# A graph layer on Trainium2: GpSimd's gathers and scatters unrolled, the scatters four groups behind, 18 dense rows a step

## The reference

```python
h = jnp.maximum(_layernorm(x, axis=-1), 0.0)
z = jnp.concatenate([h[src], h[dst], edge_attr_32], axis=-1)
m = jax.nn.sigmoid(z @ W_f + b_f) * jax.nn.softplus(z @ W_s + b_s)
message = jax.ops.segment_sum(m, src, num_segments=100000)
mean = jnp.mean(message, axis=0)
var = jnp.mean((message - mean) ** 2, axis=0)
normed = (message - mean) * jax.lax.rsqrt(var + 1e-5) * gamma + beta
return x + h + normed
```

## Time and profile before

| | us |
|---|---|
| median of 3 runs | 1177.55 |
| lowest and highest | 1175.6, 1177.74 |
| profiled execution, span | 1163.4 |
| stage one, last scatter issued until | 940.49 |
| first table load of stage two | 947.58 |

### The profile page before, as it was taken

One profiled execution on the slowest core, in us unless ns is written; L12 is line 12 of the kernel. 1 busy time (PEld: TensorE's weight loads), 2 busy tenths in 40 slices (PEclk: granted clock), 3 DMA queues, 4 the chain that ended last, 5 costly groups with the idle time before them and its releaser, 6 DMA issues. The chain is left out here.

```text
span 1163.4 us, 11837 instructions
## 1 busy us (share of the span) xinstructions
PE 734.6 (63%) x3189; PEld 547.1 (47%) x3189; DVE 714.0 (61%) x1188; ACT 502.6 (43%) x1144; POOL 730.0 (63%) x596
## 2 busy tenths in 40 slices
PE   0687786766758676766857676666857100089976
PEld 0476664655646564645636564555647100033322
DVE  1377656465655647565564756556477328999956
ACT  0477454554545354454535445453547027700000
POOL 5767878888887878888787888878766620000000
PEclk9787655666575566666566566766566555589989
DMA  7995344333434333232332323233333249749998
GB/s 275 389 362 136 64 101 76 82 79 78 98 59 99 68 71 62 43 62 41 63 43 59 61 43 61 41 63 43 61 54 46 14 163 399 327 178 386 426 428 365
DMA packets 77417, 161.95 MB, mean 139 GB/s; under 512 B 39663, under 2 KB 46159, under 8 KB 68687
## 3 DMA queue, kind: packets, MB, share of 16 engines
q1 hardware_dynamic: 22575, 80.90, 19.1%
q0 software_dynamic: 40768, 19.31, 16.1%
q10 hardware_dynamic: 14048, 61.46, 13.4%
HBM read 93.87 MB, written 67.75 MB: 139 GB/s over the span
## 5 line engine op out<-in xcount | busy, mean ns | idle before, releaser
L327 POOL DMA_INDIRECT xg<-in_x_dram,gidx x392 | 380.3, 970 | 131.5 <-issue 114.9
L339 POOL DMA_INDIRECT msgs_dram<-comb,target x196 | 348.6, 1779 | 78.1 <-issue 57.3
L408 DVE TENSOR_REDUCE row_sum<-xg 128x24 f32<-128x1536 f32 (+2 forms) x53 | 86.4, 1631 | 320.1 <-DMA xg<-in_x_dram,gidx 320.1
L550 ACT ACTIVATE sq<-xc 128x1536 f32<-128x1536 f32 (+2 forms) x53 | 73.4, 1384 | 285.1 <-DVE xc L416 259.7
L685 PE MATMUL ps_z<-ident,xc 128*128 128x128 f32 x196 | 52.6, 421 | 180.6 <-DVE xc L465 180.6
L711 PE MATMUL ps_c<-msg,same 128*128 128x64 f32 x980 | 155.3, 331 | 4.5 <-ACT same L596 4.5
L711 PEld LDWEIGHTS ps_c<-msg,same 128*128 128x128 f32 x980 | 154.9, 250 | 4.6 <-ACT same L596 4.6
L698 PEld LDWEIGHTS ps_v<-w_e,ea_t 128*128 128x128 f32 x392 | 102.2, 320 | 70.9 <-issue 70.9
L698 PE MATMUL ps_v<-w_e,ea_t 128*128 128x128 f32 x392 | 128.6, 430 | 0.0
L685 PEld LDWEIGHTS ps_z<-ident,xc 128*128 128x128 f32 x196 | 34.3, 211 | 190.9 <-DVE xc L465 190.9
L695 PE MATMUL ps_v<-b_row,ones 1*128 1x512 f32 x98 | 96.5, 1083 | 38.4 <-ACT z_t L573 38.4
(11 more groups left out here) (87 smaller groups left out, 968.0 us busy)
## 6 DMA issues: line engine op xcount, KB each, us to landing
m_buf<-msgs_dram SPq DMA_DIRECT2D x38, 1024.0 KB, 20.2
msgs_dram<-zeros ACTq DMA_DIRECT2D x16, 1536.0 KB
xg<-in_x_dram SPq DMA_DIRECT2D x48, 512.0 KB, 3.6
out_dram<-m_buf ACTq DMA_DIRECT2D x21, 1024.0 KB, 9.9
y_spill_dram<-y_kept ACTq DMA_DIRECT2D x19, 512.0 KB, 3.0
y_kept<-y_spill_dram SPq DMA_DIRECT2D x9, 1024.0 KB, 30.0
xg<-in_x_dram,gidx POOLq DMA_INDIRECT x392
msgs_dram<-comb,target POOLq DMA_INDIRECT x196, 3.3
```

The costliest lines, as they stand in the source:

```text
L327: pool.indirect_dma_start(xg[:, slot, 2 * j + c, :], None, x, bass.IndirectOffsetOnAxis(ap=gidx[:, g.slot(UNROLL), c, j:j + 1], axis=0),). ...
L339: pool.indirect_dma_start(msgs, bass.IndirectOffsetOnAxis(ap=target[:, g.slot(UNROLL), j:j + 1], axis=0), comb[:, g.slot(UNROLL), j, :], N ...
```

## The change

- GpSimd's program is written out completely: 49 steps without a loop. The gathers read their indices from the loaded table `ids`; the tile `gidx`, its copy on VectorE and the semaphores `staged` and `gathers_begun` are gone.
- Steps 7, 8 and 9 each scatter two groups, the later steps one, so that step n from 10 on scatters group n - 4. Four groups are left after the last gather.
- 18 dense rows a step instead of 16: 44 steps carry them, from step 5 to step 48, the step of the last gather. After it the other engines run 3 steps (`TAIL`) without dense rows. The layer norm instructions cover 26 rows.
- 16 groups of dense rows are spilled (288 rows) instead of 19 (304 rows). The step at which y changes from spilled to kept falls inside an iteration, which is written out on VectorE and ScalarE (`TURN`).
- The equality tiles `same` are packed: 10 of 128 columns instead of 16. The zeroing keeps its 16 rows.

```diff
-BULK = 16
+BULK = 18
+NODE_GROUPS = -(-N_ROWS // BULK)
-SKEW = 4
-STEPS = GROUPS + SKEW
+SKEW = 5
+STEPS = NODE_GROUPS + SKEW
+TAIL = 3
-SPILL = 19
-ACC_LAG = 7
+SPILL = 16
+ACC_FIRST, ACC_LAG = 7, 4
+ZERO_ROWS = 16
...
-            def gather(g):
-                slot = g.slot(SLOTS)
+            def gather(n):
+                if n >= SLOTS:
+                    pool.wait_ge(centred, n - SLOTS + 1)
                 for j in range(TILES):
                     for c in range(2):
                         pool.indirect_dma_start(
-                            xg[:, slot, 2 * j + c, :], None, x,
-                            bass.IndirectOffsetOnAxis(ap=gidx[:, g.slot(UNROLL), c, j:j + 1], axis=0),
-                        ).then_inc(gathered[slot], 16)
+                            xg[:, n % SLOTS, 2 * j + c, :], None, x,
+                            bass.IndirectOffsetOnAxis(ap=ids[:, c, n * TILES + j:n * TILES + j + 1], axis=0),
+                        ).then_inc(gathered[n % SLOTS], 16)
...
-            for u in range(2 * UNROLL):
-                step(Group(u // UNROLL, u % UNROLL))
-            with pool.Fori(2, ITERS) as it:
-                for u in range(UNROLL):
-                    step(Group(it, u))
-            for u in range(1 + ACC_LAG):
-                step(Group(ITERS, u))
+            pool.wait_ge(ids_loaded, 96)
+            begun = 0
+            for n in range(GROUPS):
+                gather(n)
+                if n == ACC_FIRST:
+                    pool.wait_ge(table_zeroed, 16 * (ZERO_PARTS + 2))
+                for _ in range(0 if n < ACC_FIRST else min(2, n - ACC_LAG + 1 - begun)):
+                    accumulate(begun)
+                    begun += 1
+            for n in range(begun, GROUPS):
+                accumulate(n)
...
-            def stage_indices(g):
-
-                dve.tensor_copy(gidx[:, g.slot(UNROLL), :, :],
-                                ids[:, :, bass.ds(g.n * TILES, TILES)]).then_inc(staged, 1)
+            def stage_sources(g):
+
...
-            for u in range(STEPS - LAST + 1):
+            for u in range(1 + TAIL):
                 step(Group(ITERS, u), False)
...
-        same = sb("same", [P, TILES, TILES, P])
+        same = sb("same", [P, PAIRS[TILES], P])
```

More of the change, by code:

```diff
@@ L40 @@
 N_REST = NODES - P * N_ROWS
-LAST_ROWS = N_ROWS - BULK * LAST
+NODE_GROUPS = -(-N_ROWS // BULK)
+LAST_ROWS = N_ROWS - BULK * (NODE_GROUPS - 1)
 UNROLL = 6
 ITERS = LAST // UNROLL
-SKEW = 4
-STEPS = GROUPS + SKEW
+SKEW = 5
+STEPS = NODE_GROUPS + SKEW
+TAIL = 3
 SLOTS = 3
-SPILL = 19
-KEPT_ROWS = (GROUPS - SPILL) * BULK
-ACC_LAG = 7
+SPILL = 16
+KEPT_ROWS = (NODE_GROUPS - SPILL) * BULK
+ACC_FIRST, ACC_LAG = 7, 4
 ZERO_PARTS = 16
 ZERO_AHEAD = 4
+ZERO_ROWS = 16
 DUMP = (TILES + 1) * P
 assert ALL_TILES == TILES * GROUPS and ITERS * UNROLL == LAST and UNROLL % SLOTS == 0
-assert 0 < LAST_ROWS < BULK
-assert (SPILL + 1 + SKEW) % UNROLL == 0
+assert 0 < LAST_ROWS < BULK and STEPS == GROUPS
+TURN = (SPILL + SKEW) // UNROLL
+PAIRS = [b * TILES - b * (b - 1) // 2 for b in range(TILES)] + [TILES * (TILES + 1) // 2]
+assert 1 <= TURN < ITERS
 S_BLK = 32
@@ L174, in stage_one @@
         upto = sb("upto", [P, P])
-        zeros = sb("zeros", [P, BULK * F])
+        zeros = sb("zeros", [P, ZERO_ROWS * F])
         w_z = sb("w_z", [P, 2 * F])
@@ L179, in stage_one @@
         own = sb("own", [P, UNROLL, TILES])
-        gidx = sb("gidx", [P, UNROLL, 2, TILES], I32)
         xg = sb("xg", [P, SLOTS, ROWS, F])
@@ L307, in load @@
                     load_edges(g)
-            run_groups(sp, load, SKEW)
+            run_groups(sp, load, 0)
         @block.gpsimd
@@ L339, in accumulate @@
                     pool.indirect_dma_start(
-                        msgs, bass.IndirectOffsetOnAxis(ap=target[:, g.slot(UNROLL), j:j + 1], axis=0),
-                        comb[:, g.slot(UNROLL), j, :], None, compute_op=ALU.add,
+                        msgs, bass.IndirectOffsetOnAxis(ap=target[:, n % UNROLL, j:j + 1], axis=0),
+                        comb[:, n % UNROLL, j, :], None, compute_op=ALU.add,
                     ).then_inc(accumulated, 16)
[L344 to L350, removed]
-                    pool.wait_ge(table_zeroed, 16 * (ZERO_PARTS + 2))
-                if g.back(ACC_LAG).exists():
-                    accumulate(g.back(ACC_LAG))
-            for u in range(2 * UNROLL):
-                step(Group(u // UNROLL, u % UNROLL))
-            with pool.Fori(2, ITERS) as it:
-                for u in range(UNROLL):
-                    step(Group(it, u))
-            for u in range(1 + ACC_LAG):
-                step(Group(ITERS, u))
+            pool.wait_ge(ids_loaded, 96)
[3 more added lines that the diff above has]
+                if n == ACC_FIRST:
+                    pool.wait_ge(table_zeroed, 16 * (ZERO_PARTS + 2))
+                for _ in range(0 if n < ACC_FIRST else min(2, n - ACC_LAG + 1 - begun)):
[3 more added lines that the diff above has]
+                accumulate(n)
             pool.wait_ge(accumulated, 16 * ALL_TILES)
@@ L489, in step @@
                 if g.back(-1).exists():
-                    stage_indices(g.back(-1))
+                    stage_sources(g.back(-1))
                 if in_steps(g.back(1)):
@@ L512, in _ @@
                 step(Group(0, u), True)
-            first_kept = (SPILL + 1 + SKEW) // UNROLL
-            with dve.Fori(1, first_kept) as it:
+            with dve.Fori(1, TURN) as it:
                 for u in range(UNROLL):
                     step(Group(it, u), True)
-            with dve.Fori(first_kept, ITERS) as it:
+            for u in range(UNROLL):
+                step(Group(TURN, u), TURN * UNROLL + u <= SPILL + SKEW)
+            with dve.Fori(TURN + 1, ITERS) as it:
                 for u in range(UNROLL):
                     step(Group(it, u), False)
-            for u in range(STEPS - LAST + 1):
+            for u in range(1 + TAIL):
                 step(Group(ITERS, u), False)
@@ L643, in _ @@
                 step(Group(0, u), True)
-            first_kept = (SPILL + 1 + SKEW) // UNROLL
-            with act.Fori(1, first_kept) as it:
+            with act.Fori(1, TURN) as it:
                 for u in range(UNROLL):
                     step(Group(it, u), True)
-            with act.Fori(first_kept, ITERS) as it:
+            for u in range(UNROLL):
+                step(Group(TURN, u), TURN * UNROLL + u <= SPILL + SKEW)
+            with act.Fori(TURN + 1, ITERS) as it:
                 for u in range(UNROLL):
                     step(Group(it, u), False)
-            for u in range(STEPS - LAST + 1):
+            for u in range(1 + TAIL):
                 step(Group(ITERS, u), False)
@@ L710, in combine @@
                     for b in range(j + 1):
-                        pe.matmul(ps_c[:, j, :], same[:, b, j, :], msg[:, b, :], start=(b == 0), stop=(b == j))
+                        pe.matmul(ps_c[:, j, :], same[:, PAIRS[b] + j - b, :], msg[:, b, :], start=(b == 0), stop=(b == j))
                 last = g.known and g.n == LAST
```

26 lines of the change are left out of this document (12 added, 14 removed).

## The result

The changed kernel took 1199.56 us (median of 4 executions, 1195.17 to 1205.03), the kernel before 1177.05 us beside it: ratio 1.0201, 95% interval [1.018, 1.0222]. It is slower, as forecast, but by 22.5 us instead of 6.3, and outside the range. Whether it is more than 2% slower, the interval leaves open.

A forecast was written before the change was run, and what follows sets the result against it. GpSimd was taken to bound stage one, never waiting there. Terms -9.0 + 30.9 - 25.3 + 10.7 - 1 = +6.3 on 1163.4 gave a span of 1169.7, plus 14.15: 1183.9 us; range 1172 to 1190.

The forecast's parts named there:

- part 2: Start of stage one: indices from ids, without gidx copy or staged wait, remove GpSimd waits; -9.0 us, range -9.5 to -6.
- the last one of the sum: Whole kernel: the 14.15 us between profiled span and median of runs carries over, 1169.7 to 1183.9 us.
- 1 unrolled: GpSimd's written-out program: unrolled steps already took as long as looped ones, so worth 0.
- 3 four behind: Steps 7 to 9 and tail: doubled scatter groups cost +30.9, the shorter tail gives -25.3; net +5.6 us.
- 4 18 rows: Steps 8 to 47: longer centring holds each third scatter 0.27 us longer; +10.7 us, bounds 0 and 16.
- 5 stage two: Packed same tile, spills and stage two's returning blocks: -1 us, between -4 and +1.
- Rival (b): Doubled steps and tail: groups cost 9.6 each and TensorE runs at full clock; 1178.9 us, no change, chance 0.14.
- Rival (a): Third scatter of each step: its hold does not grow, the 10.7 us drop out; 1173.2 us, faster, chance 0.20.
- Rival (c): Fourth scatter or first gather newly held by the y_kept sum, up to 1.26 us a step; 1234 us, chance 0.03.
- Rival (d): First scatter: the table's zeros are late and it waits 3 us; 1187 us, chance 0.07.

The follow-up runs named there:

- after_third: The changed kernel, unaltered, run a third time, beside the kernel before at 1168.5 us: 1168.81 us, ratio 0.9998.
- ids_no_wait_again: Second run of the kernel before, written out, with gathers reading ids, no gidx copy and no staged wait: ratio 0.9913.
- before_look: The kernel before, unchanged, profiled beside the third run of the changed kernel: 1167.24 us, span 1165.5.
- unroll_only: The kernel before with GpSimd's program written out for all steps and nothing else: ratio 0.9993 to the kernel before.
- lag4_second: Second run of the kernel before with indices from ids, no staged wait and scatters 4 behind, 16 dense rows: ratio 0.9929.
- The PSUM experiments: ids_no_wait with row_sum and row_rstd in PSUM (0.9862 of the kernel before), and with row_sum alone in PSUM (0.9879).
- no_wait_psum_rows: ids_no_wait with row_sum and row_rstd in PSUM, the message sum not kept (output lacks the right mean): 0.9862 of the kernel before.
- after: The changed kernel as first measured and profiled, beside the kernel before at 1177.05 us: 1199.56 us, ratio 1.0201.
- rows18_lag7: The changed kernel with gather groups 1 to 7 waiting on own_staged and scatters 7 behind again: 1.0062 of the kernel before.
- ids_no_wait: The kernel before, written out, gathers reading ids, without gidx copy and staged wait, 7 behind, 16 dense rows: ratio 0.9905.
- the early waits: The changed kernel with one wait put back, gather groups 1 to 7 waiting on own_staged: 1.0091 of the kernel before.
- after_pauses: The changed kernel with a wait for the previous gathers' landing ahead of gather groups 4 to 7: 1.0188, later 1.0167, of the kernel before.

## Why the prediction was wrong, and where it was right

**The step that failed is part 2, and with it the last one of the sum.** Part 2 said of GpSimd's new wait, on the centring of three groups back: it "is met some 13 us before it is asked for", and of the zeroed table: "the zeros have landed by then". In the result's profile gather steps 6 and 7 stand in that wait for 11.59 and 5.50 us, and the first scatter waits 18.82 us for the zeros and starts at 120.80 instead of 90.7.

The last step of the sum was "the median of the runs is 1177.55, 14.15 more, and I carry that over". In every later execution the own time is its span plus 1.7 (1199.08 and 1197.4, 1167.24 and 1165.5). So the profiled execution took about 1165.1 us, 12 us less than the runs it stood beside. By this, and by its trace (under what stays open), it was of the kind seen in five sessions, which I call the first kind; the times were of the other kind. That difference is no constant that can be carried over: it is a condition with which a change may interact, and this one did.

Part 2 (-9.0) was worked out from a trace of the first kind. There it is right: in `after_third` the centring is done 13.6 to 14.8 us before each of gather steps 3 to 7 begins (forecast 13), step 7 starts at 78.43 (forecast 79), and step 8 of `ids_no_wait_again` is 10.1 earlier than in `before_look`. On the other kind the wait that part 2 removes is replaced by a longer one, for TensorE's signals, and then by one for the zeros: the first scatter at 120.80 instead of 89.60, 31.2 us. Of these the wait for the zeros is 18.82 less 0.30. The other 12.7 are the two waits of 11.59 and 5.50 less their usual gaps (16.5), less 3.8, because in the third session some gathers were longer (up to 2.22). The last scatter ends 31.0 later (975.54 against 944.58), the span is 27.6 longer. By the medians the changed kernel is 30.8 us slower on that kind (1199.56 against 1168.81) and the kernel before 8.5 (1177.05 against 1168.54), and the difference of the two is the 22 us measured.

**The other steps, on chips of the first kind.** Counted at the end of the last scatter, one execution each:

| part | from, to | forecast | measured |
|---|---|---|---|
| 1 unrolled | before, `unroll_only` (ratio) | 0 | 0.9993 |
| 2 no wait | 938.68 to 931.17 | -9.0 | -7.5 |
| 3 four behind | 931.17 to 933.01 | +5.6 | +1.8 |
| 4 18 rows | 933.01 to 944.58 | +10.7 | +11.6 |
| 5 stage two | 226.8 to 225.2 after it | -1 | -1.6 |
| sum of spans | 1165.5 to 1169.8 | +6.3 | +4.3 |

The kernels are `before_look`, `ids_no_wait_again`, `lag4_second` and `after_third`. The medians of the third session differ by 0.3 us, with an interval of -2.3 to +1.8, while these single spans differ by 4.3; the times of one kernel scatter by some 8 us (1163.3 to 1171.6 in the third session), and stage two alone took 221.2 us in `lag4_second` and 225.2 in `after_third`, so each row is known to a few us only. By the medians part 2 gave 10.3 and 10.7 us (third and first session), and parts 3 to 5 together cost 10.6 where the forecast had 15.3. On this kind the change is "same", not "slower": that the forecast had the sign right is luck, since it came true only by the stall.

Part 2 in the table: of the 10.1 us at gather step 8, 2.0 go again in step 8 itself, where the fourth scatter takes 3.08, and step 8 20.42 instead of 18.40. That hold was not in the forecast. The first gather starts 0.9 earlier (5.06 against 5.95), not 0.2.

Part 3 was right in its mechanism and mis-sized in one term, the price of a second scatter group in a step. The windows of POOL in `lag4_second`, steps 7 to 9 and 10 to 47:

```profile
77.76:164.29 86.53, 65.26 (x49) 0.70 0.48 114
164.29:867.80 703.51, 564.51 (x456) 0.60 0.33 63
```

Steps 7 to 9 take 86.53 against 59.25 without the doubled groups (`ids_no_wait_again`): 27.3 for three groups, 9.1 each, not 10.3 (bounds 9.6 and 11). The forecast took the group price from the tail and added it to steps of 18.5; undoubled, steps 7 and 8 are 20.25 and 20.42, with holds that the doubled ones lack in part. The tail gives back 24.7 (25.3 forecast). In the changed kernel (`after_third`) steps 7 to 9 take 31.3, 28.4 and 28.3, where the forecast had 28 to 30 each. Rival (b) had this direction.

Part 4 held. The same windows of `after_third`:

```profile
78.43:166.46 88.03, 65.82 (x48) 0.64 0.44 105
166.46:879.66 713.20, 574.20 (x456) 0.60 0.33 65
```

713.20 less 703.51 is 9.7, or 0.255 a step where 0.27 stood. One step of the changed kernel (first profile), against the earlier trace rows:

```profile
529.51 1.89 DVE L410 SCALAR_TENSOR_TENSOR xc<-row_sum,xg 128x1664 f32<-128x1664 f32 x1
530.14 2.67 POOL L343 DMA_INDIRECT msgs_dram<-comb,target  x1 [0.30 <-issue]
531.32 1.88 DVE L459 SCALAR_TENSOR_TENSOR xc<-xc,row_rstd 128x1664 f32<-128x1664 f32 x1
533.12 1.54 POOL L343 DMA_INDIRECT msgs_dram<-comb,target  x1 [0.30 <-issue]
533.38 1.36 DVE L472 TENSOR_TENSOR y_kept<-xc,xg 128x1152 f32 x1 [0.18 <-DVE xc L459]
```

L410 had 1.26 left at 530.14; less 0.12 that is 1.14, and the scatter is 1.13 longer than the fourth. The same rule gives the length of all 41 such third scatters within 0.03 us, in this profile and in `after_third`; the mean third scatter took 2.71 us in both (forecast about 2.75, before 2.50). The PSUM experiments show the cause, which the prediction had only argued: with one SBUF input in place of two the same instruction holds nobody. Rival (a) is refuted. Rival (c) did not come in the changed kernel, but its mechanism is real: in `no_wait_psum_rows` the y_kept sum holds a gather (829.36, above). The Trainium skill ("SBUF — State Buffer", Who interferes with whom) puts all three on one shared port; these runs agree. The same section tells of a probe in which `tensor_tensor`, the form of the y_kept sum, did not stall a DMA; here it holds 35 gathers of `no_wait_psum_rows` by the rule above, within 0.03 us, and the measurement decides. Rival (d) was the right place (zeros and first scatter) with the wrong price, 18.5 us instead of 3, and only where the stall is.

**What stays open.** What makes a chip, or a session, of the second kind, and why TensorE's signals come late there. The traces have a mark of it: those with the stall keep 4,766 to 6,026 landing events of DMAs (five traces, the changed kernel's first among them), all others, the one of before that the forecast was read from among them, 12,974 to 13,170. Waits put down to "remote" stand only in the five, in the waits view of the first one from 30 to 125 us:

```profile
ACT spl L574 <- remote: 33.9, 1, 33.9
...
DVE not_later L426 <- remote: 28.8, 1, 28.8
...
ACT ea_t L566 <- remote: 12.9, 2, 6.9
```

Whether fewer kept events are a cause of the late signals or another effect of the same thing, no run tells.

The record of semaphores has a second mark. Of 245 signals of TensorE in stage one, every one stands within 0.02 us of the end of its matmul in each of the fifteen traces without the stall. In the five with it, 82 to 123 are more than 0.5 us late, and 70 to 110 of these belong to gather step 10 and later, late by up to 6.5 us. So the signals go on being late to the end of stage one; from step 10 on it costs GpSimd nothing (steps of 18.80 us against 18.77 in `after_third`). Some signals are missing from the record in these five; they are not counted. The guess that they come only when GpSimd stops issuing gathers has this for it: 220 of the 506 late signals belong to matmuls that end while a gather group is being issued, but only 19 arrive in such a time, though it is half of stage one; the others come while GpSimd scatters or pauses. The first long waits of `after` end 4.5, 1.7 and 1.7 us after GpSimd stops, those of `rows18_lag7` 2.9, 1.7 and 1.2 us. Against a simple form of it: other signals come on time in the midst of gathers, in the same traces, as they do in `ids_no_wait` throughout. So the guess is not shown. With pauses it was never tried on such a chip. Nor is there a profile of the kernel before there, so where it loses its 8 us is not known. What the early waits do to the stall is seen across two kinds of chip only: gather step 7 is 12.4 us later than without the stall, where the changed kernel has 13.8, but the first scatter is only 11.6 us later (110.34 against 98.78), where the changed kernel has 31.2.

## What to carry to other kernels

Compare the own time of the profiled execution with the median before any sum: 12 us between them, on a kernel that repeats to 0.3%, said that the trace and the times came from different conditions, and a change that lives on a wait at the start must be priced under both. Where a wait has no plausible end in the timeline, compare the signals in the trace with the ends of the instructions that send them. Before lengthening a VectorE instruction that covers the issue of indirect DMAs, count its SBUF inputs: with the small operand of the centring and that of the normalising in PSUM two scatters a step are free and the step is 0.6 us shorter, while with the first alone in PSUM the hold only went on to the next scatter. A price read where it occurs (a group in the tail) is not what the same work costs inside a step that has holds of its own.

## What was not expected of the hardware

- The same program took 1168.8 us in one session and 1199.6 and 1203.8 in two others, with a wait of 34 us for matmuls whose signals stand in the trace 30 us after them; the kernel before took 1168.5 beside the first of these, 1177.1 and 1175.6 beside the others.
- With the clearing running (DMA share 1.03 in `after_pauses`), the landing of a gather group was waited for 6.3 us after its last issue.
- A gather or scatter of GpSimd is held by any of three VectorE instructions with two SBUF inputs (the centring, the normalising, the sum into y_kept) in which it starts, for what is left of it less 0.12 us: 161 cases in four traces (those with over 0.2 us left), all within 0.03 us. With one input of the centring or the normalising in PSUM, none of the 116 scatters that start inside them is held.
